# A recurrence with attention: mixing with unnormalised exponentials, and a router with its loads rearranged

## The chip, the cores and the metric

The program runs on one core of a Trainium2 chip. The time is that of one launch on the device, in microseconds (us). A core has five engines with queues of their own: TensorE (PE in the profile; its weight loads are listed as PEld), VectorE (DVE), ScalarE (ACT), GpSimd (POOL) and SyncE (SP, which here only issues DMAs). They meet through semaphores.

## The reference

`x` has 4 batches of 1024 tokens of 256 features. Four layers follow each other, each adding to `x`. The first is the long one: 1024 steps in which each step needs the step before.

```python
def step(carry, x_t):                       # scanned over the 1024 tokens; batch 4, H = 256
    h0, c0, h1, c1, a = carry
    h0, c0 = _lstm_cell(concatenate([x_t, a]), h0, c0, Wi0, Wh0, bi0, bh0)
    h1, c1 = _lstm_cell(h0, h1, c1, Wi1, Wh1, bi1, bh1)
    q = h1 @ Wq.T
    attn = softmax(einsum('bh,bsh->bs', q, context))      # over 64 context rows
    mixed = einsum('bs,bsh->bh', attn, context)
    a2 = tanh(concatenate([mixed, h1]) @ Wo.T + bo)
    return (h0, c0, h1, c1, a2), a2
x = x + recurrence(layernorm(x), ctx)
x = x + ffn(layernorm(x))                   # 256 -> 1024 -> 256, quantised
x = x + attention(layernorm(x), ctx)        # 16 heads, 64 context rows
x = x + moe(layernorm(x))                   # top 1 of 8 experts, 256 -> 1024 -> 256
```

## The kernel before

Everything is float32. **The recurrence** (`scan`) holds the state turned, with features on the 128 partitions. A product of the state (4 or 8 columns, the weights of the array) with a weight matrix (64 moving columns) is split over four column groups of the array (`j` in 0 to 3) and two halves of the contraction (`k`), so it has 8 matmuls; each is two passes in float32, and the profile counts passes (x16). The result stands in PSUM with the batch on partitions 32j to 32j+3 and 64 of the 256 features in each group. DVE turns it back in blocks of 32 by 32 (`transpose`).

`Wq` and the context are folded into `kp`, and the mixed half of `Wo`, the context and `bo` into `vp`, before the recurrence begins. Since the softmax sums to one, `bo` may stand in `vp`. A step ends so:

1. PE forms `scores` (`kp`) and starts `a_sum` with `woh` times h1.
2. DVE takes the negative maximum (line 571). ACT forms the exponentials and, through its accumulator, their `total` (line 430, which is two instructions: the ACTIVATE and the reading of the accumulator).
3. DVE: the reciprocal of the total (573), the turn of the exponentials (575), the turn of the reciprocal (577), and their product `pT` (579).
4. PE adds `vp` times `pT` to `a_sum` (line 363). DVE turns `a_sum` (582), and ACT takes its tanh into `aT` (435). `aT` opens the gates of the next step (`wa`).

PE fills waits with the next step's products that need no `a`: `wh0` and `wx`. The order is written out by hand.

**The last layer** has the stages `route`, `scatter` and `experts`, each a block that ends for all engines together. `route` normalises 32 tiles of 128 tokens, forms their logits on PE, keeps the normed rows in `rows`, and then finds for each token a slot, sorted by expert. SP meanwhile fills 40 slot tiles in DRAM (`slots_x`) with blanks, loads `w1` and `w2` of all experts (8 MB each) and stores the residual to `x_rows` (4 MB). `scatter` sends the 32 tiles to their slots by indirect DMAs of POOL. `experts` works through 40 slot tiles on PE.

## Time and profile before

| | |
|---|---|
| time, median of 3 runs | 8262.45 us (8253.83 to 8263.24) |
| the profiled execution | 8255.78 us, its span 8254.0 us |
| PE busy | 6793.0 us, 82% |
| DVE busy | 4208.6 us, 51% |
| ACT busy | 3382.8 us, 41% |
| POOL busy | 313.9 us, 4% |
| DMA | 102.08 MB |

The span runs from the first to the last instruction. The recurrence lies between about 60 and 7290 us; a busy share over the span is mostly its average. In each step the engines wait for each other in turn, so that what counts is the chain through one step and not any engine's sum. The router, the scatter and the experts take the time from about 7783 us on.

### The profile page before, as it was taken

How to read it: one execution, taken by the hardware profiler on the slowest of the kernel's cores; microseconds unless marked ns; L12 is line 12 of the kernel's file. 1: busy time of each engine (PE TensorE's matmuls, PEld its weight loads, DVE VectorE, ACT ScalarE, POOL GpSimd, SP SyncE). 2: the span in 40 equal slices, each digit the busy share in tenths (PEclk: the TensorE clock that was granted, in tenths of full speed). 3: DMA queues.
4: the chain of work that ended last, by engine and by line, in shares of the span. 5: the costliest groups of instructions: out<-in, count | busy, mean ns of one | idle time of the engine just before them, and what ended most of it. 6: DMA issues, size and time to landing. Idle time of an engine off the chain costs nothing. (4 is left out here: it accounts for less than half of the span.)

```text
span 8254.0 us, 814880 instructions
## 1 busy us (share of the span) xinstructions
PE 6793.0 (82%) x380441; PEld 5788.2 (70%) x380449; DVE 4208.6 (51%) x21164; ACT 3382.8 (41%) x17073; POOL 313.9 (4%) x334
## 2 busy tenths in 40 slices
PE   7888888888888888888888888888888888868769
PEld 5777777777777777777777777777777777746546
DVE  5554555555455545455445555555555544466822
ACT  4444444444444444444444444444444444452422
POOL 0000000000000000000000000000000000002532
PEclk8999999999999999999999999999999999989889
DMA  2000000000000000000000000000000000000143
GB/s 87 5 0 0 5 0 0 0 0 5 0 0 0 5 0 0 0 2 4 0 0 0 5 0 0 0 5 0 0 0 0 5 0 0 0 14 11 70 164 109
DMA packets 94641, 102.08 MB, mean 12 GB/s; under 512 B 46570, under 2 KB 81904, under 8 KB 93424
## 3 DMA queue, kind: packets, MB, share of 16 engines
q1 hardware_dynamic: 89200, 88.73, 3.5%
q0 software_dynamic: 5376, 12.63, 0.4%
q8 instruction: 22, 0.36, 0.0%
q14 instruction: 43, 0.35, 0.0%
HBM read 79.75 MB, written 23.67 MB: 13 GB/s over the span
## 5 line engine op out<-in xcount | busy, mean ns | idle before, releaser
L353 PE MATMUL scan_sums<-rec_wh,scan_hT 128*4 128x64 f32 x131008 | 2392.3, 219 | 3.3 <-issue 3.3
L476 DVE STREAM_TRANSPOSE scan_sums<-scan_sums 128x64 f32<-128x64 f32 x6144 | 1552.2, 265 | 1126.1 <-PE scan_sums L353 1111.4
L353 PEld LDWEIGHTS scan_sums<-rec_wh,scan_hT 128*4 128x4 f32 x131008 | 1989.6, 89 | 3.8 <-issue 3.8
L353 PE MATMUL scan_sums<-rec_wa,scan_aT 128*4 128x64 f32 (+1 forms) x65536 | 1103.8, 219 | 381.7 <-ACT scan_aT L435 381.7
L353 PEld LDWEIGHTS scan_sums<-rec_wa,scan_aT 128*4 128x4 f32 (+1 forms) x65536 | 914.9, 88 | 570.6 <-ACT scan_aT L435 570.6
L353 PE MATMUL scan_sums<-rec_wx,scan_xT 128*4 128x64 f32 (+1 forms) x65536 | 1292.1, 219 | 7.2 <-issue 6.3
L353 PE MATMUL scan_sums<-rec_wi,scan_hT 128*4 128x64 f32 (+1 forms) x65536 | 1102.6, 219 | 145.0 <-issue 3.7
L353 PEld LDWEIGHTS scan_sums<-rec_wi,scan_hT 128*4 128x4 f32 (+1 forms) x65536 | 913.6, 88 | 333.7 <-DVE scan_hT L567 329.9
L353 PEld LDWEIGHTS scan_sums<-rec_wx,scan_xT 128*4 128x4 f32 (+1 forms) x65536 | 1024.2, 89 | 7.9 <-issue 6.9
L419 ACT ACTIVATE scan_tanh_f<-scan_sums 128x8 f32<-128x8 f32 x2048 | 364.0, 178 | 1216.4 <-DVE scan_sums L476 1216.4
L414 ACT ACTIVATE scan_sums<-rec_bias 128x192 f32<-128x192 f32 x2050 | 686.7, 335 | 301.2 <-PE scan_sums L393 5.7
L435 ACT ACTIVATE scan_aT<-scan_a_sum 128x8 f32<-128x8 f32 x1024 | 182.0, 178 | 1515.4 <-DVE scan_a_sum L582 1515.4
L363 PE MATMUL scan_scores<-rec_kp,scan_hT 128*4 128x64 f32 x16384 | 416.5, 219 | 377.1 <-DVE scan_hT L567 377.0
L363 PE MATMUL scan_a_sum<-rec_vp,scan_pT 128*4 128x64 f32 x16384 | 416.5, 219 | 295.8 <-DVE scan_pT L579 295.8
L363 PEld LDWEIGHTS scan_scores<-rec_kp,scan_hT 128*4 128x4 f32 x16384 | 227.6, 85 | 562.7 <-DVE scan_hT L567 562.7
L421 ACT ACTIVATE scan_scanned<-scan_sums 128x16 f32<-128x16 f32 x2048 | 397.8, 194 | 518.2 <-DVE scan_sums L476 502.0
L567 DVE SCALAR_TENSOR_TENSOR scan_hT<-scan_tanh_o,scan_sums 128x8 f32<-128x8 f32 x2048 | 333.0, 163 | 466.4 <-ACT scan_sums L426 466.4
L363 PEld LDWEIGHTS scan_a_sum<-rec_vp,scan_pT 128*4 128x4 f32 x16384 | 227.7, 85 | 481.1 <-DVE scan_pT L579 481.1
L582 DVE STREAM_TRANSPOSE scan_a_sum<-scan_a_sum 128x64 f32<-128x64 f32 x1024 | 272.4, 266 | 547.1 <-PE scan_a_sum L363 547.1
L430 ACT ACTIVATE scan_exps<-scan_scores,scan_neg_max 128x65 f32<-128x65 f32 x1024 | 324.6, 317 | 431.8 <-DVE scan_neg_max L571 431.8
L571 DVE TENSOR_REDUCE scan_neg_max<-scan_scores 128x1 f32<-128x65 f32 x1024 | 231.4, 226 | 518.7 <-PE scan_scores L363 518.7
L565 DVE TENSOR_TENSOR_SCAN scan_sums<-scan_scanned 128x24 f32<-128x24 f32 x2048 | 444.6, 217 | 68.9
(262 smaller groups left out, 6104.6 us busy)
## 6 DMA issues: line engine op xcount, KB each, us to landing
experts_bias<-in_b SPq DMA_DIRECT2D x40, 640.0 KB, 4.3
moe_w<-in_w SPq DMA_DIRECT2D x16, 1024.0 KB, 12.5
slots_x<-route_blank SPq DMA_DIRECT2D x40, 129.0 KB, 2.3
experts_x<-slots_x SPq DMA_DIRECT2D x40, 129.0 KB
w_xres<-in_x_steps SPq DMA_DIRECT2D x8, 512.0 KB, 12.8
w_xres<-in_x SPq DMA_DIRECT2D x4, 1024.0 KB, 12.1
x_rows<-w_xres SPq DMA_DIRECT2D x4, 1024.0 KB
a_rows<-scan_stage SPq DMA_DIRECT2D x224, 16.0 KB, 1.5
```

Source lines behind the costliest of these rows:

```text
L353: last = nc.tensor.matmul(sums[layer][BANK[g]][32 * j:32 * j + ROWS[g], 0:64], state[:, k, FIRST[g]:FIRST[g] + ROWS[g]], weight[:, k, j, 6 ...
L363: last = nc.tensor.matmul(bank[32 * j:32 * j + B, 0:64], state[:, k, :], weight[:, k, j, :], start=start and k == 0, stop=stop and k == 1, ...
L414: nc.scalar.activation(layer_sums[l][:, :, 0:64], w["bias"][:, l, :, :], ACT.Copy).then_inc(seeded[l], 1)
L419: nc.scalar.activation(tanh_f[l][:], gates_of[l][F][:, :, 0:B], ACT.Tanh).then_inc(f_tanh[l], 1)
L421: nc.scalar.activation(ig_terms[l], gates_of[l][IG][:, :, 0:2 * B].rearrange("p k (f b) -> p k f b", f=2), ACT.Tanh).then_inc(c_terms[l], 1)
L430: nc.scalar.activation(exps[:], scores[:, 0:S + 1], ACT.Exp, bias=neg_max[:], accum_out=total).then_inc(exps_done, 1)
L435: nc.scalar.activation(state_of(aT), a_sumT.rearrange("p (k u) -> p k u", k=2)[:, :, 0:B], ACT.Tanh).then_inc(a_ready, 1)
L476: nc.vector.transpose(turned[l][g], sums[l][g][:, 0:64]).then_inc(gates_turned[l][g], 1)
L565: nc.vector.tensor_tensor_scan(cell[l], flat[l][:, 0], flat[l][:, 1], 0.0, ALU.mult, ALU.add).then_inc(c_done[l], 1)
L567: nc.vector.scalar_tensor_tensor(state_of(hT[l]), tanh_o[l][:], 1.0, tanh_c[l].rearrange("p (k b) -> p k b", k=2), ALU.add, ALU.mult).then ...
L571: nc.vector.tensor_reduce(neg_max[:], scores[:, 0:S + 1], AX.X, ALU.max, negate=True).then_inc(max_done, 1)
L582: nc.vector.transpose(a_sumT, a_sum[:, 0:64]).then_inc(a_turned, 1)
```

## The change

In the recurrence the exponentials are no longer multiplied by the reciprocal before the product. They are turned as they are, and PE multiplies them by `vp` in a product of its own, `mixed`. The totals come from PE too: the turned exponentials, as weights, against a column of ones, which leaves each batch's total on the partitions where `mixed` has that batch. DVE has copied the `woh` part out of `a_sum` (`from_h`) in the meantime. After the products it forms mixed / total + from_h in one instruction, in SBUF (`a_natural`), and turns that. ACT forms no total any more. One gate of `wx` (G, 8 matmuls) moves behind the products.

Outside the steps, the 40 blank tiles are written at the recurrence's beginning. In `route`, SP stores `x_rows` first and then loads `w1`; `w2` is loaded in `scatter`. The copy of the normed tile into `rows` moves from DVE to ACT, which forms it two buffers behind the normalisation.

```diff
-        total = scores[:, 128:129]
+        mixed, spread_total = scores[:, 192:256], a_sum[:, 256:257]
@@ SP, scan
                 sp.dma_start(ffn["b_in"][:], ins["b_in"]).then_inc(ffn["x_in"], 16)
+                sp.wait_ge(blank_made, 1)
+                for n in range(SLOT_TILES):
+                    sp.dma_start(slots_x[P * n:P * n + P, :], blank[:]).then_inc(blanked, 16)
+                sp.wait_ge(blanked, 16 * SLOT_TILES)
                 sp.wait_ge(restored, FC)
@@ PE, scan
-                    head_product(scores, state_of(hT[1]), w["kp"], True, True).then_inc(scores_done, 1)
-                    head_product(a_sum, state_of(hT[1]), w["woh"], True, False)
+                    head_product(scores, state_of(hT[1]), w["kp"]).then_inc(scores_done, 1)
+                    head_product(a_sum, state_of(hT[1]), w["woh"]).then_inc(h_summed, 1)
                     if not last:
                         product(0, hT[0], w["wh0"], (GATE_O,))
                         pe.wait_ge(x_ready, n + 1)
-                        product(0, xT[(s + 1) % 2], w["wx"], (GATE_F, GATE_I, GATE_G))
-                    pe.wait_ge(probs_ready, n)
-                    head_product(a_sum, pT[:], w["vp"], False, True).then_inc(a_summed, 1)
+                        product(0, xT[(s + 1) % 2], w["wx"], (GATE_F, GATE_I))
+                    pe.wait_ge(h_kept, n)
+                    pe.wait_ge(exps_turned, n)
+                    for k in range(2):
+                        for j in range(4):
+                            last_total = nc.tensor.matmul(spread_total[32 * j:32 * j + B, :], expsT[:, k, 0:B], ones[:],
+                                                          start=k == 0, stop=k == 1, skip_group_check=True)
+                    last_total.then_inc(total_spread, 1)
+                    head_product(mixed, expsT[:, :, 0:B], w["vp"]).then_inc(a_terms, 1)
                     if not last:
-                        product(0, xT[(s + 1) % 2], w["wx"], (GATE_O,))
+                        product(0, xT[(s + 1) % 2], w["wx"], (GATE_G, GATE_O))
@@ ACT, scan
-                    nc.scalar.activation(exps[:], scores[:, 0:S + 1], ACT.Exp, bias=neg_max[:],
-                                         accum_out=total).then_inc(exps_done, 1)
+                    nc.scalar.activation(exps[:], scores[:, 0:S], ACT.Exp, bias=neg_max[:]).then_inc(exps_done, 1)
@@ DVE, scan
+                    dve.wait_ge(h_summed, n)
+                    nc.vector.tensor_scalar(from_h[:], a_sum[:, 0:64], 1.0, None, ALU.mult).then_inc(h_kept, 1)
                     dve.wait_ge(exps_done, n)
-                    nc.vector.reciprocal(inv[:], total).then_inc(inv_done, 1)
-
-                    nc.vector.transpose(expsT[:].rearrange("p k s -> p (k s)"), exps[:, 0:S]).then_inc(p_turned, 1)
-                    dve.wait_ge(inv_done, n)
-                    nc.vector.transpose(invT[:], inv[:].broadcast_to([P, 32])).then_inc(p_turned, 1)
-                    dve.wait_ge(p_turned, 2 * n)
-                    nc.vector.tensor_tensor(pT[:], expsT[:, :, 0:B], invT[:, None, 0:B].broadcast_to([P, 2, B]),
-                                            ALU.mult).then_inc(probs_ready, 1)
-                    dve.wait_ge(a_summed, n)
-                    nc.vector.transpose(a_sumT, a_sum[:, 0:64]).then_inc(a_turned, 1)
+                    nc.vector.transpose(expsT[:].rearrange("p k s -> p (k s)"), exps[:]).then_inc(exps_turned, 1)
+
+                    dve.wait_ge(total_spread, n)
+                    nc.vector.reciprocal(inv[:], spread_total).then_inc(a_terms, 1)
+                    dve.wait_ge(a_terms, 2 * n)
+                    nc.vector.scalar_tensor_tensor(a_natural[:], mixed, inv[:], from_h[:], ALU.mult, ALU.add).then_inc(a_scaled, 1)
+                    dve.wait_ge(a_scaled, n)
+                    nc.vector.transpose(a_sumT, a_natural[:]).then_inc(a_turned, 1)
@@ SP, route
-                sp.wait_ge(zeroed, 2)
-                with sp.Fori(0, SLOT_TILES) as j:
-                    sp.dma_start(slots_x[bass.ds(j * P, P), :], blank[:]).then_inc(filled, 16)
+                for b in range(B):
+                    sp.dma_start(x_rows[b].rearrange("(g p) d -> p g d", p=P), xres[:, :, b, :]).then_inc(w["x_kept"], 16)
                 for e in range(E):
                     sp.dma_start(w["w1"][:, e, :, :], ins["w1"][e].rearrange("(c p) n -> p c n", p=P)).then_inc(w["loaded"], 16)
-                for e in range(E):
-                    sp.dma_start(w["w2"][:, e, :, :], ins["w2"][e].rearrange("(f p) n -> p f n", p=P)).then_inc(w["loaded"], 16)
-                for b in range(B):
-                    sp.dma_start(x_rows[b].rearrange("(g p) d -> p g d", p=P), xres[:, :, b, :]).then_inc(w["x_kept"], 16)
-                sp.wait_ge(filled, 16 * SLOT_TILES)
@@ ACT, route
+                def keep_normed(g, b):
+                    act.wait_ge(xn_done, B * g + b + 1)
+                    nc.scalar.activation(rows[:, bass.ds(g * B + b, 1), 0:D].rearrange("p n d -> p (n d)"), xn_tile[b % 2][:],
+                                         ACT.Copy).then_inc(xn_kept, 1)
+                in_steps(act, [(deviation, 0), (keep, 1), (keep_normed, 1)])
@@ DVE, route
-                in_steps(dve, [(keep_normed, 2), (moments, 0), (normalize, 1), (keep_logits, 3)])
+                in_steps(dve, [(moments, 0), (normalize, 1), (keep_logits, 3)])
@@ SP, scatter; PE, experts
+            for e in range(E):
+                sp.dma_start(w["w2"][:, e, :, :], ins["w2"][e].rearrange("(f p) n -> p f n", p=P)).then_inc(w["loaded_down"], 16)
+                    pe.wait_ge(w["loaded_down"], 16 * E)
```

PE's instructions at the end of a step were these before, one row for each run of matmuls with its tile, weight and shape (weight columns x moving columns) and what the first waits for:

```order
L363 MATMUL scan_a_sum<-rec_woh,scan_hT 4x64 x8
L353 MATMUL scan_sums<-rec_wh,scan_hT 4x64 x8
L353 MATMUL scan_sums<-rec_wx,scan_xT 4x64 [waits scan_x_ready]
L353 MATMUL scan_sums<-rec_wx,scan_xT 4x64 x7
L353 MATMUL scan_sums<-rec_wx,scan_xT 8x64 x16
L363 MATMUL scan_a_sum<-rec_vp,scan_pT 4x64 [waits scan_probs_ready]
L363 MATMUL scan_a_sum<-rec_vp,scan_pT 4x64 x7
L353 MATMUL scan_sums<-rec_wx,scan_xT 4x64 x8
```

And they are these now, in the same place:

```order
L370 MATMUL scan_a_sum<-rec_woh,scan_hT 4x64 x8
L360 MATMUL scan_sums<-rec_wh,scan_hT 4x64 x8
L360 MATMUL scan_sums<-rec_wx,scan_xT 4x64 [waits scan_x_ready]
L360 MATMUL scan_sums<-rec_wx,scan_xT 4x64 x7
L360 MATMUL scan_sums<-rec_wx,scan_xT 8x64 x8
L397 MATMUL scan_a_sum<-scan_ones,scan_expsT 4x1 [waits scan_exps_turned,scan_h_kept]
L397 MATMUL scan_a_sum<-scan_ones,scan_expsT 4x1 x7
L370 MATMUL scan_scores<-rec_vp,scan_expsT 4x64 x8
L360 MATMUL scan_sums<-rec_wx,scan_xT 8x64 x8
L360 MATMUL scan_sums<-rec_wx,scan_xT 4x64 x8
```

Eight matmuls with one moving column stand between the wait and the product with `vp`, and eight of `wx` have moved behind that product.

DVE's instructions from the maximum to the turn of `a_sum` were, before:

```order
L571 TENSOR_REDUCE scan_neg_max<-scan_scores 128x1 [waits scan_scores_done]
L573 RECIPROCAL scan_inv<-scan_scores 128x1 [waits scan_exps_done]
L575 STREAM_TRANSPOSE scan_expsT<-scan_exps 128x64
L577 STREAM_TRANSPOSE scan_invT<-scan_inv 128x32 [waits scan_inv_done]
L579 TENSOR_TENSOR scan_pT<-scan_expsT,scan_invT 128x8 [waits scan_p_turned]
L582 STREAM_TRANSPOSE scan_a_sum<-scan_a_sum 128x64 [waits scan_a_summed]
```

Now they are:

```order
L587 TENSOR_REDUCE scan_neg_max<-scan_scores 128x1 [waits scan_scores_done]
L589 TENSOR_SCALAR scan_from_h<-scan_a_sum 128x64 [waits scan_h_summed]
L591 STREAM_TRANSPOSE scan_expsT<-scan_exps 128x64 [waits scan_exps_done]
L594 RECIPROCAL scan_inv<-scan_a_sum 128x1 [waits scan_total_spread]
L596 SCALAR_TENSOR_TENSOR scan_a_natural<-scan_scores,scan_inv,scan_from_h 128x64 [waits scan_a_terms]
L598 STREAM_TRANSPOSE scan_a_sum<-scan_a_natural 128x64 [waits scan_a_scaled]
```

The reciprocal and an instruction over all 64 columns now stand behind PE's products, where one turn stood alone; one turn stands ahead of them, where there were four instructions.

## Rows read from the trace of the kernel before

**Rows 1.** Windows: span, busy (count) of PE, PEld, DVE, ACT, POOL; clock, DMA share, GB/s

```profile
60.00:7290.00 7230.00, 6017.79 (x376785) 5267.23 (x376785) 3655.92 (x19731) 3029.27 (x16392) 20.62 (x56) 1.00 0.01 2
```

**Rows 2.** Instructions of line 435: duration min/median/max in ns, first and last start

```profile
L435 ACT ACTIVATE scan_aT<-scan_a_sum x1024: 177/178/178, 78.2 to 7285.5; 128x8 f32<-128x8 f32 x171
```

**Rows 3.** Timeline of one step's end: start, duration, engine, [idle before <-releaser]

```profile
3000.08 0.41 PE L363 MATMUL scan_a_sum<-rec_woh,scan_hT 128*4 128x64 f32 x16
...
3000.33 0.23 DVE L571 TENSOR_REDUCE scan_neg_max<-scan_scores 128x1 f32<-128x65 f32 x1 [0.53 <-PE scan_scores L363]
...
3000.59 0.32 ACT L430 ACTIVATE scan_exps<-scan_scores,scan_neg_max 128x65 f32<-128x65 f32 x1 [0.42 <-DVE scan_neg_max L571]
3000.80 0.16 ACT L430 ACTIVATION_READ_ACCUMULATOR scan_exps<-scan_scores,scan_neg_max 128x1 f32 x1
3001.00 0.17 DVE L573 RECIPROCAL scan_inv<-scan_scores 128x1 f32<-128x1 f32 x1 [0.45 <-ACT scan_exps L430]
3001.08 0.23 DVE L575 STREAM_TRANSPOSE scan_expsT<-scan_exps 128x64 f32<-128x64 f32 x1
3001.23 0.18 DVE L577 STREAM_TRANSPOSE scan_invT<-scan_inv 128x32 f32<-128x32 f32 x1
3001.45 0.17 DVE L579 TENSOR_TENSOR scan_pT<-scan_expsT,scan_invT 128x8 f32<-128x8 f32 x1
...
3001.66 0.41 PE L363 MATMUL scan_a_sum<-rec_vp,scan_pT 128*4 128x64 f32 x16 [0.29 <-DVE scan_pT L579]
...
3002.14 0.27 DVE L582 STREAM_TRANSPOSE scan_a_sum<-scan_a_sum 128x64 f32<-128x64 f32 x1 [0.53 <-PE scan_a_sum L363]
3002.44 0.18 ACT L435 ACTIVATE scan_aT<-scan_a_sum 128x8 f32<-128x8 f32 x1 [1.47 <-DVE scan_a_sum L582]
```

**Rows 4.** Timeline of PE, two narrower stretches of the same product: passes begun so far

```profile
3001.66 0.24 PE L363 MATMUL scan_a_sum<-rec_vp,scan_pT 128*4 128x64 f32 x4 [0.29 <-DVE scan_pT L579]
...
3001.66 0.29 PE L363 MATMUL scan_a_sum<-rec_vp,scan_pT 128*4 128x64 f32 x8 [0.29 <-DVE scan_pT L579]
```

**Rows 5.** Groups by form: busy us, mean ns of one, idle before and its releaser

```profile
L363 PE MATMUL scan_a_sum<-rec_vp,scan_pT 128*4 128x64 f32 x16384 | 416.5, 219 | 295.8 <-DVE scan_pT L579 295.8
...
L430 ACT ACTIVATE scan_exps<-scan_scores,scan_neg_max 128x65 f32<-128x65 f32 x1024 | 324.6, 317 | 431.8 <-DVE scan_neg_max L571 431.8
...
L113 ACT ACTIVATE route_norm_std<-route_norm_mean_var,route_norm_eps 128x1 f32<-128x1 f32 x32 | 9.3, 290 | 4.2 <-DVE route_norm_mean_var L99 4.2
...
L567 DVE SCALAR_TENSOR_TENSOR scan_hT<-scan_tanh_o,scan_sums 128x8 f32<-128x8 f32 x2048 | 333.0, 163 | 466.4 <-ACT scan_sums L426 466.4
...
L582 DVE STREAM_TRANSPOSE scan_a_sum<-scan_a_sum 128x64 f32<-128x64 f32 x1024 | 272.4, 266 | 547.1 <-PE scan_a_sum L363 547.1
L575 DVE STREAM_TRANSPOSE scan_expsT<-scan_exps 128x64 f32<-128x64 f32 x1024 | 232.2, 227 | 0.0
...
L1023 DVE SCALAR_TENSOR_TENSOR w_xres<-output_summed,output_back,w_xres 128x256 f32 x24 | 11.5, 479 | 0.7 <-issue 0.7
```

**Rows 6.** Instructions of line 96, router stage: first and last start

```profile
L96 DVE BATCH_NORM_STATS2 route_norm_stats<-w_xres x32: 420/423/426, 7786.6 to 7836.8; 128x6 f32 x28, 128x6 f32<-128x256 f32 x4
```

**Rows 7.** Timeline of DVE in the router's loop

```profile
7836.58 0.30 DVE L1333 COPY moe_rows<-route_xn_tile 128x256 f32 x1
7836.80 0.42 DVE L96 BATCH_NORM_STATS2 route_norm_stats<-w_xres 128x6 f32 x1
```

**Rows 8.** Windows of the router: its tile loop, and after DVE has ended

```profile
7786.50:7841.70 55.20, 43.00 (x192) 39.81 (x192) 46.23 (x256) 20.49 (x65) 0.00 (x0) 0.50 0.72 259
...
7853.60:7869.00 15.40, 0.00 (x0) 0.00 (x0) 0.00 (x0) 0.00 (x0) 0.00 (x0) 0.50 1.10 361
```

**Rows 9.** Timeline of the router's end

```profile
7853.33 0.18 DVE L1388 CAST moe_expert<-route_expert_f 128x40 int32<-128x40 f32 x1
7855.95 11.81 SPq L1249 DMA_DIRECT2D x_rows<-w_xres  x4
7869.07 1.31 POOL L1398 DMA_INDIRECT slots_x<-moe_rows,moe_slot  x1 [83.50 <-PEq L1394]
```

More of the change, by code:

```diff
@@ L289, in scan @@
         state_of = lambda tile: tile[:, :, B:2 * B]
-        exps, expsT, invT = m.sbuf("exps", [P, S + 1]), m.sbuf("expsT", [P, 2, 32]), m.sbuf("invT", [P, 32])
-        pT = m.sbuf("pT", [P, 2, B])
-        neg_max, inv = m.sbuf("neg_max", [P, 1]), m.sbuf("inv", [P, 1])
+        exps, expsT = m.sbuf("exps", [P, S]), m.sbuf("expsT", [P, 2, 32])
+        from_h, a_natural = m.sbuf("from_h", [P, 64]), m.sbuf("a_natural", [P, 64])
+        neg_max, ones, inv = m.sbuf("neg_max", [P, 1]), m.sbuf("ones", [P, 1]), m.sbuf("inv", [P, 1])
         gates_summed = [[m.sem(f"summed_{g}{l}") for g in ("f", "ig", "o")] for l in range(2)]
@@ L296, in scan @@
                                                                for n in ("f_tanh", "c_terms", "c_done", "c_kept", "h_factors", "h_ready"))
-        (a_ready, x_ready, scores_done, max_done, exps_done, p_turned, probs_ready, a_summed, inv_done, a_turned, a_kept, zeroed) = (
-            m.sem(n) for n in ("a_ready", "x_ready", "scores_done", "max_done", "exps_done", "p_turned", "probs_ready", "a_summed",
-                               "inv_done", "a_turned", "a_kept", "zeroed"))
+        (a_ready, x_ready, scores_done, max_done, exps_done, exps_turned, h_summed, h_kept, total_spread, a_terms, a_scaled, a_turned,
+         a_kept, zeroed) = (m.sem(n) for n in (
+             "a_ready", "x_ready", "scores_done", "max_done", "exps_done", "exps_turned", "h_summed", "h_kept", "total_spread",
+             "a_terms", "a_scaled", "a_turned", "a_kept", "zeroed"))
         opened = m.sem("opened")
+        blank = m.sbuf("blank", [P, ROW])
+        blank_made, blanked = m.sem("blank_made"), m.sem("blanked")
         ROWS_OUT = 16 * B * 4 * 2
@@ L358, in product, with head_product @@
                             last.then_inc(done[BANK[g]], 1)
-                def head_product(bank, state, weight, start, stop):
+                def head_product(bank, state, weight):
                     for k in range(2):
@@ L363, in head_product @@
                             last = nc.tensor.matmul(bank[32 * j:32 * j + B, 0:64], state[:, k, :], weight[:, k, j, :],
-                                                    start=start and k == 0, stop=stop and k == 1, skip_group_check=True)
+                                                    start=k == 0, stop=k == 1, skip_group_check=True)
                     return last
@@ L466, in _ @@
                 nc.vector.memset(zeros[:], 0.0)
+                nc.vector.memset(ones[:], 1.0)
                 nc.vector.memset(scores[:, 0:S], 0.0)
@@ L471, in _ @@
                 dve.wait_ge(a_ready, 1)
-                nc.vector.memset(pT[:], 0.0).then_inc(zeroed, 1)
+                nc.vector.memset(mixed, 0.0)
+                nc.vector.memset(spread_total, 1.0).then_inc(zeroed, 1)
                 def turn(l, g, n):
@@ L1229, in route @@
         rank, count = m.psum("rank"), m.psum("count")
-        loaded, zeroed, filled, const, xn_done, turned_done, xT_done, sum_done, logits_done, step, exp_done, counted = (
-            m.sem(n) for n in ("loaded", "zeroed", "filled", "const", "xn_done", "turned_done", "xT_done", "sum_done", "logits_done", "step",
+        loaded, const, xn_done, turned_done, xT_done, sum_done, logits_done, step, exp_done, counted = (
+            m.sem(n) for n in ("loaded", "const", "xn_done", "turned_done", "xT_done", "sum_done", "logits_done", "step",
                                "exp_done", "counted"))
@@ L1388, in _, with scatter @@
                 then(nc.vector.tensor_copy(expert[:], expert_f[:]), k + 15)
-def scatter(nc, rows, slot, slots_x):
+def scatter(nc, ins, rows, slot, slots_x, w):
     sent = Pool(nc, None, "scatter").sem("sent")
     with nc.Block() as block:
+        @block.sync
+        def _(sp):
+            for e in range(E):
+                sp.dma_start(w["w2"][:, e, :, :], ins["w2"][e].rearrange("(f p) n -> p f n", p=P)).then_inc(w["loaded_down"], 16)
         @block.gpsimd
@@ L1629, in build @@
                 route(nc, ins, xres, rows, slot, expert, slots_x, x_rows, w)
-                scatter(nc, rows, slot, slots_x)
+                scatter(nc, ins, rows, slot, slots_x, w)
             experts(nc, ins, expert, slots_x, x_rows.rearrange("b t d -> (b t) d"), out.rearrange("b t d -> (b t) d"), w)
```

22 lines of the change are left out of this document (10 added, 12 removed).

## The prediction

> **What bounds the kernel now.** I read the windows first. The recurrence takes 7230 of 8254 us, with TensorE's clock at its full level, and no engine is full: PE is busy 6018 us of it, DVE 3656, ACT 3029 [rows 1]. PE's share is of little meaning, since it fills waits with products that the next step needs anyway. The last tanh of a step starts 1024 times between 78.2 and 7285.5 us, so a step takes 7.045 us [rows 2]. A time that is one chain through 1024 equal steps is read in one step: 10 ns in the chain are 10.2 us, 0.12% of the kernel.
>
> Then the timeline of a step. From the exponential's start (3000.59) to the tanh's start (3002.44) there are 1.85 us in which each row starts just after the one before has ended; this is the stretch that is rewritten [rows 3]. PE has been idle 0.29 us before `vp`, so it isn't the late one. What stands ahead of the exponential and behind the tanh is as it was.
>
> **Prices of a hand-over**, all read from the same rows: from the end of a DVE or ACT instruction to the start of one that waits for it on DVE or ACT 0.03 us (the reduction starts at 3000.33 and takes 0.23, the exponential starts at 3000.59; the turn of `a_sum` ends at 3002.41, the tanh starts at 3002.44). From DVE to PE 0.05 (`pT` ends at 3001.61 or 3001.62, PE starts at 3001.66). From the start of a product of 8 matmuls to the start of its reader on DVE 0.48 (3001.66 to 3002.14) [rows 3].
>
> **The new chain**, with the exponential's start as zero:
>
> - The exponential takes 0.317 [rows 5]. It has 64 columns for 65, which is nothing. Before, DVE waited for the reading of the accumulator, which ends at 3000.96, 0.05 behind the exponential itself [rows 3]. Now it starts at 0.317 + 0.033 = 0.350.
> - The turn of the exponentials takes 0.227 [rows 5] and ends at 0.577. PE starts at 0.628. The copy `from_h` is not in its way: `woh` starts at 3000.08 and can be read 0.48 later, at 3000.56, when the reduction has just ended; DVE's instructions over 64 columns take at most 0.27 [rows 3], so it is done by 3000.83, and the turn starts at 3000.94. PE is there too: it went idle at 3001.37, and has 8 matmuls fewer ahead, 0.22, while it is wanted at 3001.22.
> - The totals, 8 matmuls or 16 passes over one column. No row of before has one. The bounds: a pass lasts 219 ns [rows 5] and four passes end after 0.24, so that the fourth begins about 0.02 after the first, 7 ns apart; with the next four the end is at 0.29 [rows 4], and 16 end after 0.41, so that the 16th begins at 0.19 [rows 3]. That reads as four column groups side by side, each busy some 55 ns with a pass over 64 columns, while the next pass on another group can begin 7 ns later. With one column only the 7 ns are left: 16 x 7 = 0.11. The upper bound is the pace of 64 columns, 16 / 15 x 0.19 = 0.20, or 0.22 with the pause between fours. I take 0.11, since what holds back the fifth pass looks like columns.
> - `mixed` starts at 0.738, and its reader at 1.214. The reciprocal runs beside it: the last pass of the totals begins at 0.628 + 0.10, its result can be read at most 0.29 later (0.48 less 0.19), so the reciprocal starts by 1.02, takes 0.17 [rows 3] and is handed on at 1.22. A tie; I add nothing, with 0.01 as the bound.
> - The new instruction over 128x64, with a pointer for the scalar and PSUM for one input. Over 128x8 and without pointer it takes 163 ns, over 128x256 with pointer and PSUM 479 [rows 5]. A straight line between the two has 1.27 ns a column, (479 - 163) / 248, and gives 0.234; but a pointer costs once and not by the column, so the slope is less. With an estimated 1.04 the short row gives 0.163 + 0.058 = 0.22 without pointer, and the long row 0.479 - 0.200 = 0.28 with it. These are the bounds; I take 0.28, since the long row has the same operands: end 1.494, next start 1.529.
> - The turn from SBUF into PSUM: 0.227 where both ends are in SBUF, 0.266 where both are in PSUM [rows 5]. I take 0.248: end 1.777, tanh at 1.810.
>
> So 1.85 becomes 1.81: 0.042 less a step, **43 us** less over 1024. The small gain is a difference of large parts: PE starts at 0.628 where it was 1.076 (0.448 less), and then the totals (0.11) and the instruction over 64 columns with its hand-over (0.315) come in, with 0.018 back from the second turn. The bounds of the sum: all low ones together give 0.12 less, 126 us; all high ones 0.11 more, about 108 us slower.
>
> **The last layer.** DVE's last instruction of the router starts at 7853.33, but SP goes on issuing until 7867.76, and POOL's first scatter is at 7869.07 [rows 9]; no engine works in these 15 us, and DMA moves 361 GB/s [rows 8]. The blanks (5 MB) and `w2` (8 MB) leave this stage, and with 12 MB from 7784 on SP is done well before DVE even at the 259 GB/s of the tile loop [rows 8] (49 us, 7833). So the router ends 14.3 us earlier. In the tile loop DVE is busy 46.2 of 55.2 us, and PE 43.0, at half clock [rows 8]. The tiles start from 7786.6 to 7836.8, 1.62 apart [rows 6]. The copy costs DVE 0.22 from its start to the next [rows 7]; without it 1.40 a tile is left, and PE's share of 43.0 / 32 = 1.34 allows it. 31 x 0.22 = 6.8; I take 6 (bounds 0 and 7), since the loop's ends stay. Together **20 us**. In the scatter `w2` (23 us at 361 GB/s) has done before POOL's 32 issues have, which needed the 45 us to 7914; hidden, and uncovered it would give back at most the whole 20.
>
> **The rest.** At the recurrence's start SP issues 40 more DMAs, behind the loads that DVE needs in its third step, and DVE clears a few tiles more. The engines fetch code by DMA too there, so I put 2 us, at most 10.
>
> The sum: 8255.8 - 43 - 20 + 2 = 8195. The profiled execution is 7 us below the median of the three, and they lie 9 us apart; I put half of that back and say **8198**. What a measurement of this kernel can tell from no change is 0.2%, 16.5 us.
>
> **The rivals.**
>
> 1. *The forecast*, 0.60, with 8150 to 8225 for its own range.
> 2. *A pass over one column isn't short.* Then the totals take 0.22, the step becomes 0.068 longer, 70 us, and the time 8198 + 43 + 70 = 8311: slower. It decides from a pass pace of about 0.15 on, where the recurrence gives back the last layer's gain. For it: no one-column pass stands in the trace, and there may be a floor for weights and columns together. Against it: the 7 ns within four passes, with a weight load for each. The Trainium skill (TensorEngine Tiling (Array Packing), Instruction Overhead) says that a matmul over one column has the latency of one over 60. No run here shows it yet; the fours at 7 ns are the reason why I don't follow it, and by that rule the kernel would be slower than before, as in this rival. Chance 0.14.
> 3. *In between*: passes at 9 to 11 ns, or both DVE instructions at their high ends, 8220 to 8280. Chance 0.16.
> 4. *The exponential gets shorter without its accumulator.* 0.317 is long for 65 columns. If the 0.09 over a plain pass goes with it, the time is 8198 - 92 = 8106. Against it: the square root over one column, with a pointer for its bias and without accumulator, takes 0.290 [rows 5], so it is the pointer, which stays. Chance 0.05.
> 5. *The DMAs collide*: `w2` slows the scatter, or the blanks slow the recurrence's first steps, and 20 of 20 us are lost: 8218. Chance 0.05.
>
> The Trainium skill (TensorE: Matmul & The Clock Gate, Back-to-back issue gap) gives a floor of about 25 ns between matmuls with few columns. Taken for each column group it is four passes in 25 ns, the 0.11 above; taken for all passes it would be 0.40 for the totals, which the 7 ns between passes contradict.
>
> **How the numbers follow.** From 8140 to 8300 the range leaves out rival 4 and most of rival 2. Faster by over 0.2% (below 8246) are 1, 4, 5 and half of 3: 0.75 after taking a little off; within 0.2% falls most of the other half, 0.08; slower is 2 and the rest, 0.17.
>
> **What would show it.** In the profile of the changed kernel: a step's period (7.045 now) of 7.00; PE idle for 0.2 to 0.3 us before the first one-column pass; from the first of them to the first pass of `mixed` 0.11 and not 0.22; the exponential still at 0.317; the instruction over 64 columns at 0.28; the reciprocal ending at about the time when `mixed` can be read; POOL's first scatter about 20 us nearer to the router's start, and PE not waiting for `w2`. The prediction is wrong if the totals hold back `mixed` longer, if the 64-column copy delays the turn of the exponentials, or if the tiles of the router stay 1.6 us apart.

## The result

The changed kernel takes **8321.31 us** in the median (8318.54 to 8327.2, four runs) against 8261.23 of the kernel before (8253.83 to 8263.24, four runs): ratio 1.0073, 95% interval 1.006 to 1.0086. It is slower by 0.7%, where 8198 was predicted, and it lies outside the range of 8140 to 8300. The profiled execution has a span of 8320.5 us, 66.5 more than before.

Where the 66.5 us lie is read from first and last starts. These are the last tanh of a step, the statistics at the head of the router's tiles, and the router's end, in the changed kernel:

```profile
L447 ACT ACTIVATE scan_aT<-scan_a_sum x1024: 177/178/178, 77.1 to 7366.9; 128x8 f32<-128x8 f32 x171
```

```profile
L96 DVE BATCH_NORM_STATS2 route_norm_stats<-w_xres x32: 422/426/429, 7870.1 to 7917.3; 128x6 f32 x28, 128x6 f32<-128x256 f32 x4
```

```profile
7933.92 0.18 DVE L1397 CAST moe_expert<-route_expert_f 128x40 int32<-128x40 f32 x1
7934.59 12.31 SPq L1407 DMA_DIRECT2D moe_w<-in_w  x5
7935.45 1.31 POOL L1412 DMA_INDIRECT slots_x<-moe_rows,moe_slot  x1 [66.61 <-PEq L1403]
```

The 1023 periods of the recurrence took 7207.3 us before [rows 2] and take 7289.8 now: 82.5 more. From the first statistics to POOL's first scatter there were 82.5 us [rows 6, 9], and there are 65.35 now: 17.1 less. What lies before, between and after changes by 1 us in all. So the last layer's half of the change gave nearly what it should, and the recurrence gave back nearly five times as much.

The end of a step, in the timeline of the changed kernel (start, duration, engine):

```profile
3003.33 0.41 PE L370 MATMUL scan_a_sum<-rec_woh,scan_hT 128*4 128x64 f32 x16
...
3003.58 0.23 DVE L587 TENSOR_REDUCE scan_neg_max<-scan_scores 128x1 f32<-128x65 f32 x1 [0.53 <-PE scan_scores L370]
...
3003.80 0.23 DVE L589 TENSOR_SCALAR scan_from_h<-scan_a_sum 128x64 f32<-128x64 f32 x1
3003.84 0.31 ACT L443 ACTIVATE scan_exps<-scan_scores,scan_neg_max 128x64 f32<-128x64 f32 x1 [0.42 <-DVE scan_neg_max L587]
3004.19 0.24 DVE L591 STREAM_TRANSPOSE scan_expsT<-scan_exps 128x64 f32<-128x64 f32 x1 [0.16 <-ACT scan_exps L443]
3004.55 0.19 PEld L397 LDWEIGHTS scan_a_sum<-scan_ones,scan_expsT 128*4 128x4 f32 x16 [0.32 <-issue]
3004.58 0.26 PE L397 MATMUL scan_a_sum<-scan_ones,scan_expsT 128*4 128x1 f32 x16 [0.17 <-DVE scan_expsT L591]
...
3004.68 0.41 PE L370 MATMUL scan_scores<-rec_vp,scan_expsT 128*4 128x64 f32 x16
...
3004.92 0.17 DVE L594 RECIPROCAL scan_inv<-scan_a_sum 128x1 f32<-128x1 f32 x1 [0.49 <-PE scan_a_sum L397]
3005.15 0.28 DVE L596 SCALAR_TENSOR_TENSOR scan_a_natural<-scan_scores,scan_inv,scan_from_h 128x64 f32<-128x64 f32 x1
3005.47 0.26 DVE L598 STREAM_TRANSPOSE scan_a_sum<-scan_a_natural 128x64 f32<-128x64 f32 x1
3005.76 0.18 ACT L447 ACTIVATE scan_aT<-scan_a_sum 128x8 f32<-128x8 f32 x1 [1.61 <-DVE scan_a_sum L598]
```

From the exponential to the tanh there are 1.92 us, where 1.85 stood before [rows 3] and 1.81 was predicted. The totals, which rival 2 suspected, are short: their first pass is at 3004.58, the first of `mixed` at 3004.68. The loss stands one row earlier. The turn of the exponentials ends at 4.19 + 0.245 = 3004.43, and PE's first pass follows 0.14 later, where DVE's results reached PE in 0.05 before. And the weight load in front of it (PEld) names no engine that it waited for: its idle time ended by "issue", which is the profile's word for time in which it sees no engine being waited for. Over the whole run it is the same, in the groups by form (busy us, mean ns of one, then the idle time before them and what ended it):

```profile
L397 PEld LDWEIGHTS scan_a_sum<-scan_ones,scan_expsT 128*4 128x4 f32 x16384 | 194.6, 83 | 331.4 <-issue 330.5 <-DVE scan_from_h L589 0.9
```

Line 394 is the second of the two waits written ahead of the totals. It stands in the trace as an instruction of its own, on the queue of PE's weight loads, once a step (the first wait, line 393, has no row):

```profile
L394 PEldq EVENT_SEMAPHORE  x1024: 51/51/51, 75.6 to 7365.4; - x171
```

In a typical step (the offsets are from the exponential's start) the turn ends at 590 ns; the semaphore instruction is recorded 40 ns later with 51 ns, the weight load starts 75 ns behind its start, and the first pass 31 ns behind that: 146 ns in all, where the hand-over of `pT` took 53 in the kernel before. The theory for the experiments: **a second wait ahead of PE's weight load stands alone, and when it is the one that comes last, some 0.09 us a step are lost behind it**, 93 us in all.

### The profile page after: what moved, and what is told of

Its sections match the earlier page's. It is cut to its first block and busy times, and to the rows that moved or that the text cites. A ratio compares the mean times of both kernels' runs of the same rounds, so it can differ in the third digit from the quotient of the medians.

```text
span 8320.5 us, 847492 instructions
## 1 busy us (share of the span) xinstructions
PE 6899.0 (83%) x396825; PEld 5925.1 (71%) x396833; DVE 4540.5 (55%) x21136; ACT 3323.8 (40%) x16081; POOL 311.7 (4%) x332
## 5 line engine op out<-in xcount | busy, mean ns | idle before, releaser
L443 ACT ACTIVATE scan_exps<-scan_scores,scan_neg_max 128x64 f32<-128x64 f32 x1024 | 321.5, 314 | 431.3 <-DVE scan_neg_max L587 431.3
L594 DVE RECIPROCAL scan_inv<-scan_a_sum 128x1 f32<-128x1 f32 x1024 | 173.0, 169 | 508.3 <-PE scan_a_sum L397 508.3
L397 PEld LDWEIGHTS scan_a_sum<-scan_ones,scan_expsT 128*4 128x4 f32 x16384 | 194.6, 83 | 331.4 <-issue 330.5
L370 PE MATMUL scan_scores<-rec_vp,scan_expsT 128*4 128x64 f32 x16384 | 418.4, 217 | 0.0
```

The source lines that it names most:

```text
L370: last = nc.tensor.matmul(bank[32 * j:32 * j + B, 0:64], state[:, k, :], weight[:, k, j, :], start=k == 0, stop=k == 1, skip_group_check=True)
L397: last_total = nc.tensor.matmul(spread_total[32 * j:32 * j + B, :], expsT[:, k, 0:B], ones[:], start=k == 0, stop=k == 1, skip_group_check ...
L443: nc.scalar.activation(exps[:], scores[:, 0:S], ACT.Exp, bias=neg_max[:]).then_inc(exps_done, 1)
```

## The experiments

Each kernel was timed beside the kernel before on the same chip. That had medians of 8255.51 us beside experiments 1, 2, 4 and 5, 8256.71 beside 3, 6, 7 and 8, and 8255.94 beside 9 and 10; beside the changed kernel it had 8261.23. So a difference between an experiment and the changed kernel is uncertain by some 6 us, and is given by the ratios too where it matters. "Period" is the median distance of the last tanh's starts (7.033 us before, 7.100 in the changed kernel; the 7.045 of the prediction is the mean with the slow first and last steps). Ratios are to the kernel before, with 95% intervals.

### 1. One wait for both

```diff
-                    pe.wait_ge(h_kept, n)
-                    pe.wait_ge(exps_turned, n)
+                    pe.wait_ge(exps_turned, 2 * n)
@@ DVE
-  nc.vector.tensor_scalar(from_h[:], a_sum[:, 0:64], 1.0, None, ALU.mult).then_inc(h_kept, 1)
+  nc.vector.tensor_scalar(from_h[:], a_sum[:, 0:64], 1.0, None, ALU.mult).then_inc(exps_turned, 1)
```

> The changed kernel with one edit: the copy from_h and the turn of the exponentials count up the same semaphore, and PE waits for that one (2n) instead of for two. My theory: in the changed kernel the second of PE's two waits stands as an instruction of its own ahead of the first weight load, and the way from the end of the turn to PE's first pass was 0.15 us where a single wait gives 0.05. It expects 0.095 less a step: the exponential to the tanh 1.826 (1.921 now), a step 7.005 (7.100 now), the time 8321 - 97 = 8224. Rival: the first one-column pass, or weights that were just turned, or PE's pause start late whatever the waits are; then the step stays at 7.10 and the time at 8321.

Measured: 8230.04 us (8228.43 to 8237.92), ratio 0.997 (0.9958 to 0.9983); period 7.006, exponential to tanh 1.834. The same work in the same order, with one semaphore for two, is 91 us faster than the changed kernel (85 by the two ratios), and faster than the kernel before. In the traces the hand-over is 0.055 us for 0.146, and the way from the exponential to the tanh is 0.087 a step shorter, 89 us. The row of the weight load now names the turn again, and its idle time is 0.06 us a step shorter:

```profile
L396 PEld LDWEIGHTS scan_a_sum<-scan_ones,scan_expsT 128*4 128x4 f32 x16384 | 164.3, 83 | 267.3 <-DVE scan_expsT L590 267.3
```

### 2. The kernel before, with a second wait

The wait on `max_done` is met 1 us before `probs_ready`; it orders nothing new. It only makes `probs_ready` the second of two. No pass over one column is in this kernel, so the experiment also tests the rival that such a pass starts late.

```diff
+                    pe.wait_ge(max_done, n)
                     pe.wait_ge(probs_ready, n)
```

> The kernel before with one line more: ahead of PE's wait for pT it waits for the maximum, which is long done. It changes nothing that is computed, and the one-column passes are not in it. The theory of the second wait expects 0.095 more a step, 97 us: 8261 + 97 = 8358, with PE's first weight load of vp about 0.12 behind the end of pT's instruction, where it was 0.05. The rival (the one-column passes start late) expects 8261, within 4 us.

Measured: 8344.92 us (8343.36 to 8346.49), ratio 1.0108 (1.0091 to 1.0125); period 7.115. One line that orders nothing costs 89 us. In the step the product starts 147 ns behind the end of `pT` instead of 52; exponential to tanh is 90 ns longer, the period 82. The row of the load of `vp` shows it as above, "issue" where it said DVE scan_pT:

```profile
L363 PEld LDWEIGHTS scan_a_sum<-rec_vp,scan_pT 128*4 128x4 f32 x16384 | 257.6, 85 | 546.5 <-issue 546.5
```

### 3. The two waits in the other order

```diff
-                    pe.wait_ge(h_kept, n)
-                    pe.wait_ge(exps_turned, n)
+                    pe.wait_ge(exps_turned, n)
+                    pe.wait_ge(h_kept, n)
```

> The changed kernel with TensorE's two waits written in the other order: first for the turned exponentials, then for the kept product; both semaphores stay. Theory (a wait costs when it stands as an instruction of its own AND is the one that comes last; the first-written of two rides in the weight load): the standing wait is now the early one, but it is written behind the late one, so what stands in front of the load decides. If the late wait rides in the load and the early one stands ahead of it, satisfied for long, nothing is lost: hand-over 0.05 to 0.06 us, period 7.006, about 8230 us, as with one wait (8230.04). Rival (any second wait costs, whichever comes last): hand-over 0.146, period 7.10, about 8321 us.

Measured: 8234.07 us (8231.97 to 8240.29), ratio 0.9974 (0.9964 to 0.9984); exponential to tanh 1.834, as with one wait; period 7.015. Both semaphores and both waits are still there, and the semaphore instruction too (its line, and the group of the weight load):

```profile
L394 PEldq EVENT_SEMAPHORE  x1024: 51/51/51, 76.6 to 7273.9; - x171
```

```profile
L397 PEld LDWEIGHTS scan_a_sum<-scan_ones,scan_expsT 128*4 128x4 f32 x16384 | 163.9, 83 | 267.8 <-DVE scan_expsT L591 267.8
```

Line 394 is now the wait for `h_kept`, met long before: it runs at 229 ns, while the exponential is still at work. The wait that comes last is written first and rides in the weight load. So the rival (any second wait costs) falls: what costs is the late wait standing alone. Two lines swapped are worth 87 us (83 by the ratios).

### 4. The totals over 64 columns

One wait as in experiment 1, and the column of ones 64 wide; the reciprocal reads the first column.

```diff
-        mixed, spread_total = scores[:, 192:256], a_sum[:, 256:257]
+        mixed, spread_total = scores[:, 192:256], a_sum[:, 256:320]
-        neg_max, ones, inv = m.sbuf("neg_max", [P, 1]), m.sbuf("ones", [P, 1]), m.sbuf("inv", [P, 1])
+        neg_max, ones, inv = m.sbuf("neg_max", [P, 1]), m.sbuf("ones", [P, 64]), m.sbuf("inv", [P, 1])
-                    nc.vector.reciprocal(inv[:], spread_total).then_inc(a_terms, 1)
+                    nc.vector.reciprocal(inv[:], spread_total[:, 0:1]).then_inc(a_terms, 1)
```

> As e1, but the totals are formed over 64 columns of ones instead of one (DVE still takes one of them). If columns set the pace, from the first pass of the totals to the first of mixed it takes 0.22 instead of 0.10, and the time is e1's plus 0.125 x 1024 = 128: 8352 if e1 is 8224. If a pass over one column costs as much as one over 64 (the second rival of the prediction), it is e1's time, and the 0.10 is seen in both.

Measured: 8359.44 us (8356.65 to 8363.05), ratio 1.0126 (1.0109 to 1.0143); period 7.138. From the first pass of the totals to the first of `mixed` there are 0.22 us, in the timeline of PE:

```profile
3002.84 0.41 PE L396 MATMUL scan_a_sum<-scan_ones,scan_expsT 128*4 128x64 f32 x16
3003.06 0.41 PE L370 MATMUL scan_scores<-rec_vp,scan_expsT 128*4 128x64 f32 x16
```

With one column it is 0.103. The 129 us between this run and experiment 1 are what columns cost here (exponential to tanh 1.957 for 1.834, which is 126 us), and rival 2 is refuted as a mechanism, though its time (8311) is the nearest to the measured one.

### 5. The blanks later in the recurrence

The changed kernel, with SP's 40 blanks behind the write of `w_out` instead of ahead of it.

```diff
-                sp.wait_ge(blank_made, 1)
-                for n in range(SLOT_TILES):
-                    sp.dma_start(slots_x[P * n:P * n + P, :], blank[:]).then_inc(blanked, 16)
-                sp.wait_ge(blanked, 16 * SLOT_TILES)
                 sp.wait_ge(restored, FC)
                 sp.dma_start(w_out_scratch, raw[:, 1, :, :]).then_inc(ffn["w_out_kept"], 16)
                 sp.wait_ge(ffn["w_out_kept"], 16)
+                sp.wait_ge(blank_made, 1)
+                for n in range(SLOT_TILES):
+                    sp.dma_start(slots_x[P * n:P * n + P, :], blank[:]).then_inc(blanked, 16)
+                sp.wait_ge(blanked, 16 * SLOT_TILES)
```

> The changed kernel with the 40 blank tiles issued behind the store of w_out, some 200 us into the recurrence, instead of at its beginning. If the blanks' DMAs delay the code that PE fetches in the first step (its period was 21.9 us, 9.8 in the kernel before), the first period comes back to about 10 and the time is 12 us less: 8309. Rival: PE's code is longer and its straight part stalls by itself; then the first period stays above 15 and the time within 4 us of 8321.

Measured: 8319.23 us (8316.11 to 8320.28), ratio 1.0077 (1.006 to 1.0093), and a span 6 us shorter. The mechanism is there: the recurrence's first period falls from 21.9 to 11.5 us (before: 9.8), since PE stands still less while the first DMAs run. The waits between 72 and 105 us, in the changed kernel and then in this one:

```profile
PEld scan_sums L360 <- issue: 15.0, 4, 4.2
PE scan_sums L360 <- issue: 14.3, 4, 4.0
```

```profile
PEld scan_sums L360 <- issue: 5.7, 4, 2.7
...
PE scan_sums L360 <- issue: 4.7, 3, 2.5
```

The time did not follow by the 10 us: 2 in the median, within what the runs scatter, and by the ratios nothing. The trace shows where most of it went. SP writes the blanks from 278 to 299 us now, and the steps of that stretch are long. SP's row and the tanh's starts:

```profile
277.97 21.49 SPq L340 DMA_DIRECT2D slots_x<-scan_blank  x40
```

```profile
280.17 0.18 ACT L447 ACTIVATE scan_aT<-scan_a_sum 128x8 f32<-128x8 f32 x1 [1.61 <-DVE scan_a_sum L598]
...
290.70 0.18 ACT L447 ACTIVATE scan_aT<-scan_a_sum 128x8 f32<-128x8 f32 x1 [2.20 <-DVE scan_a_sum L598]
...
300.48 0.18 ACT L447 ACTIVATE scan_aT<-scan_a_sum 128x8 f32<-128x8 f32 x1 [1.83 <-DVE scan_a_sum L598]
...
308.12 0.18 ACT L447 ACTIVATE scan_aT<-scan_a_sum 128x8 f32<-128x8 f32 x1 [1.61 <-DVE scan_a_sum L598]
```

These are periods of 10.5, 9.8 and 7.6 us for 7.1, and PE's loads of `scan_sums` stand still by "issue" again, 4.3 us in nine pieces. So 6.7 of the 10.4 us were lost again there: the stall moved with the blanks.

### 6. The other half alone

The step of the kernel before, with the rest of the change (blanks in the recurrence as in experiment 5, loads around the router, the copy on ScalarE).

```diff
@@ SP, scan
                 sp.wait_ge(ffn["w_out_kept"], 16)
+                sp.wait_ge(blank_made, 1)
+                for n in range(SLOT_TILES):
+                    sp.dma_start(slots_x[P * n:P * n + P, :], blank[:]).then_inc(blanked, 16)
```

> The kernel before with the change's other half alone: slots blanked in the recurrence (here behind the write of w_out), loads of the experts' weights around the router, the copy of the normalised rows on ScalarE; the recurrence's step as before. Theory (the loads' part gained 17 us from the router to the scatter, less 2 us ahead of the router, and was only hidden by the step's loss): period 7.033, exponential to tanh 1.852 as before, last layer 17 shorter, 8238 to 8245 us. Rival (the blanks' DMAs beside the recurrence, or the loads around the router, cost what they give): 8255 or more.

Measured: 8245.14 us (8241.35 to 8247.53), ratio 0.9984 (0.9975 to 0.9993): 11.6 us faster, of the 17 that stand between router and scatter. What is missing lies in the recurrence, which is 9.2 us longer in the trace (7216.5 for 7207.3, in a span 9.7 shorter): three periods of 8.4, 9.4 and 8.1 us while the blanks are written, as in experiment 5, cost 4.8, and some 5 come from the period, which is 7.038 for 7.033 with the same instructions.

### 7. One wait, and the blanks late

The edits of experiments 1 and 5 together.

```diff
-                    pe.wait_ge(h_kept, n)
-                    pe.wait_ge(exps_turned, n)
+                    pe.wait_ge(exps_turned, 2 * n)
@@ SP, behind the write of w_out
+                for n in range(SLOT_TILES):
+                    sp.dma_start(slots_x[P * n:P * n + P, :], blank[:]).then_inc(blanked, 16)
```

> One wait on TensorE for both, and the blanks behind the write of w_out. Theory (the two gains add up; the long first period of 21 us shrinks to about 11.5 us): 8219 to 8228 us, period 7.006. Rival (the stall at the start only moves elsewhere, as the 2 us that came of it with two waits says): 8230 us, the same as with one wait alone.

Measured: 8234.58 us (8229.54 to 8237.67), ratio 0.9973 (0.9962 to 0.9983): not faster than experiment 1. The first period fell, as expected, from 21.1 to 11.2 us. But the expected rival, that the stall only moves elsewhere, is there too: three periods beside the blanks take 10.9, 8.1 and 7.7 us, 5.6 above three others. And the period of the other steps is 7.015 for 7.006, 9 us over the run. Together that is more than was won. Exponential to tanh is 1.834 in both. The 9 ns come in ahead of the exponential, where no instruction differs; most of them, 6, in front of one DVE instruction of the second layer (the scan, 3783 for 3777 ns after the tanh). The changed kernel and experiment 3 have 3783 too, but the later blanks are not what makes it: experiment 5 has 3779, experiment 2 has 3778, and the kernel before 3787. What makes it is open; it means that two builds whose steps are alike can differ by 10 us, and that a gain of the later blanks can't be claimed from the times.

### 8. The accumulator again, and PE only spreads its column

Of the path from the turn to `mixed` the 16 passes of the totals are left. Here ACT sums the rows again, into an SBUF column; PE spreads that with four small matmuls (four columns of the identity as weights) while DVE is still turning the exponentials. The blanks are late and each product has one wait.

```diff
+                    pe.wait_ge(exps_done, 2 * n)
+                    for j in range(4):
+                        last_total = nc.tensor.matmul(spread_total[32 * j:32 * j + B, :], w["ident"][:, 0:100:33], total[:],
+                                                      start=True, stop=True, skip_group_check=True)
+                    last_total.then_inc(total_spread, 1)
+                    pe.wait_ge(exps_turned, n)
-                    for k in range(2):
-                        for j in range(4):
-                            last_total = nc.tensor.matmul(spread_total[32 * j:32 * j + B, :], expsT[:, k, 0:B], ones[:],
-                                                          start=k == 0, stop=k == 1, skip_group_check=True)
@@ ACT
-                    nc.scalar.activation(exps[:], scores[:, 0:S], ACT.Exp, bias=neg_max[:]).then_inc(exps_done, 1)
+                    nc.scalar.activation(exps[:], scores[:, 0:S], ACT.Exp, bias=neg_max[:], accum_out=total[:]).then_inc(exps_done, 1)
@@ DVE
-                    nc.vector.tensor_scalar(from_h[:], a_sum[:, 0:64], 1.0, None, ALU.mult).then_inc(h_kept, 1)
-                    dve.wait_ge(exps_done, n)
+                    nc.vector.tensor_scalar(from_h[:], a_sum[:, 0:64], 1.0, None, ALU.mult).then_inc(exps_done, 1)
+                    dve.wait_ge(exps_done, 2 * n)
```

> As the run before, but the totals come from ScalarE's accumulator again: the exponential sums its rows into an SBUF column, TensorE spreads that column with four passes of columns of the identity (rows 0, 33, 66, 99) while VectorE turns the exponentials, and the eight passes over a column of ones are gone. Theory (only the turn, the mixing passes and what follows stay on the path; the turn starts 0.06 later for the accumulator's reading, the 0.10 of totals leaves the path): exponential to tanh 1.80 us against 1.834, period 6.97, 8185 to 8195 us. Rival (the accumulator's reading and its hand-over cost the 0.10 again, or the reciprocal comes late because its wait is now for passes issued next to the turn): 8220 to 8230 us.

Measured: **8216.53 us** (8209.49 to 8218.93), ratio 0.9948 (0.9935 to 0.9962); period 7.000, exponential to tanh 1.824. In the timeline the spreading runs beside the turn, and the reciprocal is done before `mixed` can be read:

```profile
3000.05 0.31 ACT L442 ACTIVATE scan_exps<-scan_scores,scan_neg_max 128x64 f32<-128x64 f32 x1 [0.42 <-DVE scan_neg_max L587]
3000.27 0.19 ACT L442 ACTIVATION_READ_ACCUMULATOR scan_exps<-scan_scores,scan_neg_max 128x1 f32 x1
3000.49 0.25 DVE L591 STREAM_TRANSPOSE scan_expsT<-scan_exps 128x64 f32<-128x64 f32 x1 [0.25 <-ACT scan_exps L442]
...
3000.51 0.22 PE L395 MATMUL scan_a_sum<-scan_total,w_ident 128*4 128x1 f32 x8
...
3000.79 0.41 PE L370 MATMUL scan_scores<-rec_vp,scan_expsT 128*4 128x64 f32 x16
3000.79 0.17 DVE L594 RECIPROCAL scan_inv<-scan_a_sum 128x1 f32<-128x1 f32 x1
...
3001.26 0.28 DVE L596 SCALAR_TENSOR_TENSOR scan_a_natural<-scan_scores,scan_inv,scan_from_h 128x64 f32<-128x64 f32 x1 [0.30 <-PE scan_scores L370]
```

It beats both kernels, but not by what was expected: 0.010 a step from exponential to tanh, for 0.034. The 0.103 of totals left the path, and 0.09 came back: the turn starts 436 ns behind the exponential's start for 346, since the accumulator's reading takes 193 ns into SBUF where it took 164 into PSUM, and ends at 405. So the rival was nearly right about the size, and the gain over experiment 7 (18 us) is 15 from the period.

### 9 and 10. Why the turn of the exponentials takes 0.245 us for 0.227

Experiment 8, with the tile of exponentials 65 columns wide, of which 64 are used as in the kernel before; and then (experiment 10, whose edit is shown) with `a_natural` 65 wide too.

```diff
-        exps, expsT = m.sbuf("exps", [P, S]), m.sbuf("expsT", [P, 2, 32])
-        from_h, a_natural = m.sbuf("from_h", [P, 64]), m.sbuf("a_natural", [P, 64])
+        exps, expsT = m.sbuf("exps", [P, S + 1]), m.sbuf("expsT", [P, 2, 32])
+        from_h, a_natural = m.sbuf("from_h", [P, 64]), m.sbuf("a_natural", [P, 65])
```

> The kernel with the accumulated totals, and its tile of exponentials 65 columns wide instead of 64 (64 used, as the slice that the kernel before turned). The turn of the exponentials took 0.227 us before and 0.245 in the changed kernel, over the same 128x64. Theory A (the tile's width or place in SBUF does it): the turn takes 0.227 again, the step 0.018 less, period 6.982, about 8198 us against 8216.5. Theory B (it is that VectorE starts the turn out of an idle time, where before it began while the reciprocal was still in flight): the turn stays at 0.245, 8215 to 8218 us.

> As the run before, and the tile a_natural 65 columns wide too, whose turn into PSUM takes 0.259 us. Theory A (width): 0.24 for it, another 0.018 a step, about 8180 us. Theory B: 0.259 as before, 8215 to 8218 us.

Measured: 8215.57 us (8212.98 to 8218.59), ratio 0.9952 (0.9938 to 0.9966), and 8210.51 us (8209.25 to 8212.87), ratio 0.9945 (0.9931 to 0.9958); both have the period of experiment 8, 7.000. Both turns keep their lengths in both runs; in experiment 10:

```profile
L598 DVE STREAM_TRANSPOSE scan_a_sum<-scan_a_natural 128x64 f32<-128x64 f32 x1024 | 266.2, 260 | 35.6
L591 DVE STREAM_TRANSPOSE scan_expsT<-scan_exps 128x64 f32<-128x64 f32 x1024 | 250.9, 245 | 254.5 <-ACT scan_exps L442 254.2 <-DVE scan_from_h L589 0.3
```

The width does nothing. What is left of the two theories is that the turn was shorter because it began while the reciprocal was in flight: it takes 0.225 to 0.227 in the three kernels where it does (the kernel before, experiments 2 and 6), and 0.245 in all others, where it starts out of an idle time. The gates' turns (PSUM to PSUM) don't show such a difference, 266 against 265 ns, so this was made likely and not shown. The 5 us between the two runs have no counterpart in the step.

## Why the prediction was wrong, step by step

- **Prices of a hand-over: "From DVE to PE 0.05"; the step that failed.** The price was right for the kernel before, where PE has one wait ahead of `vp`. I carried it over to a place with two. Measured: 0.146 with the late wait second, 0.055 with one wait, 0.054 with the late wait first. The missing 0.09 a step is 91 us by experiment 1 and 87 by experiment 3 (85 and 83 by the ratios), and 89 by experiment 2, which was timed beside its own kernel before. I had the second wait before my eyes, in the bracket of PE's row that names two semaphores, and asked only whether it was met in time. It was. That does not make it free: it makes the other one stand alone.
- **Totals 0.11.** Measured 0.103 (3004.58 to 3004.68 in the timeline). The reading of the fours was right; experiment 4 has 0.22 with 64 columns, which was the upper bound. The Trainium skill (TensorEngine Tiling (Array Packing), Instruction Overhead) says that a matmul over one column has the latency of one over 60. As a pace for passes in a row on four column groups it doesn't hold here: 0.103 for 16 with one column against 0.223 with 64.
- **Exponential 0.317, turn's start 0.350.** Measured 0.314 and 0.346. That its length comes from the pointer and not from the accumulator holds: 0.313 in experiments 1 and 8, without and with accumulator.
- **Turn 0.227.** Measured 0.245: mis-sized by 0.018, with experiments 9 and 10 on its cause.
- **`from_h` not in the way.** Right: it ends at 3004.03, the turn starts at 3004.19. But PE is idle for only 0.08 us before the totals with one wait (0.17 in the changed kernel), where the signs asked for 0.2 to 0.3; the prediction's own times, 0.22 off an end at 3001.37, gave 0.07.
- **Product to reader 0.476, reciprocal a tie.** Right: in experiment 1 0.472 from the first pass of `mixed` (0.749) to the reader (1.221), with the reciprocal ending at 1.159.
- **The instruction over 64 columns 0.28.** Measured 0.284; from it to the 479 ns over 256 columns there are 1.02 ns a column, by the estimate 1.04. **The second turn 0.248:** measured 0.259, 0.011 more.
- **The sum of the step.** Without the failed hand-over the chain would be 1.826 by these terms, and 1.834 was measured with one wait: 0.024 above the forecast, of which the two turns are 0.029. So even without the failed hand-over the recurrence would have given some 18 us from this stretch (0.018 a step) and not the 43 of the forecast. The upper bound was also added up too high: totals 0.11, turn 0.018 and tie 0.01 above the forecast of -0.042 make 0.096, 98 us, and not 0.11 and 108. The bound had no term for a hand-over.
- **The last layer, 20.** Measured 17. The blanks and `w2` have left as reckoned, and the experts start no later (from POOL's first scatter to PE's first work there 47.8 us, 47.7 before). Of the copy's 6 us only 3 came: the tiles begin 47.2 us apart, first to last, for 50.2. In half of the tiles PE became the late one, at the half clock. The waits of DVE for it, in the kernel before between 7786.5 and 7841.7 us and in the changed one between 7870 and 7922, say so (us in total, times, longest),

```profile
DVE route_logits L1338 <- PE route_summed L1290: 1.9, 3, 0.8
```

```profile
DVE route_logits L1348 <- PE route_summed L1297: 6.5, 16, 1.1
```

  with PE busy 40.8 of the window's 52.3 us and DVE 39.2:

```profile
7870.00:7922.30 52.30, 40.84 (x192) 38.95 (x192) 39.17 (x224) 28.79 (x96) 0.00 (x0) 0.50 0.64 235
```

  I had allowed for PE by its share of busy time a tile, 1.34; a share says nothing of the waits between PE's own products.
- **The rest, 2.** The first period alone is 12 us longer, above my bound of 10. Experiment 5 shows that it comes with the blanks, and that 6.7 us of it only move when they are written later (5.6 in experiment 7). Its size isn't fixed: in experiment 3, with the blanks early, the first two periods take 13.1 and 9.3 us, for 21.9 and 7.3 in the changed kernel.

With the terms as measured the sum is 8255.8 - 18 (the chain, one wait) + 93 (the late second wait) - 17 + 12 = 8326, against 8321.31. The rival that came nearest in time, rival 2 with 8311, has another mechanism, which experiment 4 refutes; its time is near by chance. None of mine was a wait that stands alone.

## What to carry to other kernels

When an edit gives a matmul a second semaphore to wait for (other engines were not tried), price it, even if it is met long before. Write the wait that comes last first, or let both producers add to one semaphore, and look in the profile for "issue" ahead of an instruction that surely waits for another engine. And if a chain's gain is a small difference of large parts, as here 0.042 of 0.448, each hand-over in it is a term of the same size as the gain, and is to be read for its new place and not for the old one.

## What the runs showed of the hardware

- A second wait ahead of a matmul is an instruction of its own on PE's queue, recorded with 51 ns. Being the late one it takes the hand-over from 0.05 to 0.146 us; being met early it leaves it at 0.054 (0.055 with one wait), and the two times, 8234.07 and 8230.04 us, have overlapping intervals of their ratios.
- Passes over one column, on four column groups in turn: 16 in 0.103 us, 6.4 ns each, so four in 26 ns. Over 64 columns they need 0.223. A single pass over one column is recorded with 163 ns, one over 64 with 216 to 219.
- PE's weight loads stood still for 15.0 us in four pieces ("issue") at the start of the recurrence while SP's loads and blanks ran, and for 5.7 with the blanks later (6.0 in the kernel before). With 5 MB of blanks written at 278 us, 200 us into the recurrence, three steps lost 6.7 us. That this is the fetching of code was not measured.
- Reading the accumulator takes 193 ns into SBUF and 164 into PSUM.
- Kernels with the same instructions in a step differ by up to 9 ns a step, 9 us a run (experiments 1 and 7).
